# A sixteen-graph network on one core: VectorE centres and scales the normalisations by row blocks, one mask bias tile per graph, and the order of waits

## The chip, the cores and the metric

The kernel runs on one core of one Trainium2 chip. The metric is the device time of one execution in microseconds (us), lower is better. Before the change it is 888.2 us, the median of three runs (886.36 to 890.27).

## The reference

Sixteen graphs of 512 nodes with 64 channels pass four residual layers. `adj` is a dense 512 by 512 matrix per graph, about 6% of it non-zero. Cut to what matters:

```python
def _layernorm(x, axis=-1, eps=1e-05):
    m = jnp.mean(x, axis=axis, keepdims=True)
    v = jnp.var(x, axis=axis, keepdims=True)
    return (x - m) / jnp.sqrt(v + eps)
...
h = jnp.maximum(_layernorm(x, axis=-1), 0.0)
x = x + _L0_gnn_ref(h, adj, ...)   # Chebyshev, 4 orders: three propagations by adj
h = jnp.maximum(_layernorm(x, axis=-1), 0.0)
x = x + _L1_gnn_ref(h, adj, ...)   # encode, two masked attention layers, a 3-layer MLP
h = jnp.maximum(_layernorm(x, axis=-1), 0.0)
x = x + _L2_gnn_ref(h, adj, ...)   # GCN: relu(norm_adj @ h @ kernel)
h = jnp.maximum(_layernorm(x, axis=-1), 0.0)
x = x + _L3_gnn_ref(h, adj)        # adj @ h, then one where it exceeds 0.5, else zero
...
# in an attention layer:
att = softmax(scores * mask - NEG * (1.0 - mask), axis=2)
```

So each graph has four normalisations, each over 64 channels of 512 rows, each followed by a maximum with zero.

## The kernel before

Rows of a graph lie in four blocks of 128 on the 128 partitions (RB = 4). A tile `[P, RB, C]` is 128 partitions by 256 numbers: a row has 64 channels in each of the four blocks.

**Order of the work.** Each engine runs steps in an order written out by hand in the table `ORDER`, one list per engine. An entry `norm_gcn-2` is the step norm_gcn of the graph that entered two rounds ago. A round works on three graphs: the youngest (0) is in the Chebyshev layer, the next (1) in the two attention layers, the oldest (2) in the last attention's end, the MLP, the GCN and the last layer. There are 18 rounds, 14 of them with three graphs. The change leaves three of these lists as they are and takes one entry out of GpSimd's (called POOL in the rows).

The part of VectorE's list (DVE in the rows) that matters, in a round: stats_cheb-0, invert.2-2, norm_cheb-0, split_at0-0 to split_at3-0, attend.2-2, mask0.1-1, mask1.1-1, cheb_ht-0, mask2.1-1, ..., attend.1-1, norm_gcn-2, cheb_fold2-0, gcn_fold-2, stats_last-2, mask0.2-1, cheb_fold1-0, stats_enc-0, norm_last-2, mask1.2-1, norm_enc-0, mask2.2-1, enc_ht-0, mask3.2-1, last_fold-2.

GpSimd's list: norm_cheb-0, add_cheb_bias-0, split_qk.1-1, mask_bias.1-1, inverse_roots-0, cheb_u3-0, norm_gcn-2, mask_bias.2-1, split_qk.2-1, cheb_f0-0, norm_last-2, norm_enc-0, add_mlp_bias-0.

**A normalisation.** VectorE makes mean and variance (`norm_stats`, L685 to L691). GpSimd raises variance plus eps to the power -0.5 (L414, `rstd`), then subtracts the mean from all rows at once (L417, `centred`, 128x256). VectorE then takes the maximum with zero and multiplies by `rstd` in one operation over the 256 numbers of a partition (L698; for the GCN L831, with `rstd` times `dinv` of L828). For the two layers of the young graph (tiles `_pre`) the result is copied once more (L706), so that one transpose on TensorE (L908) puts it on both halves of the partitions. For the two layers of the old graph (tiles `_post`) it is split into a high part in fp32r and a low remainder (`split_u`, L726 and L728), which TensorE multiplies by the adjacency (`propagate`, L936).

**The mask.** `mask_rows` multiplies a block of scores in PSUM by the adjacency (L795), then adds the bias tile `gate` and takes the row maximum in one operation that writes SBUF (L803). `gate` is 0 where there is an edge of weight one and -NEG where there is none: GpSimd makes it from the adjacency (L480, 128x2048), once for each of the two attention layers, though it is the same for both.

**GpSimd's other operations** near them: L428 adds a bias to x (`x_b`), L486 makes the low parts of queries and keys (`q_lo`, `k_lo`), L438 to L448 make roots of the row sums, L454 to L462 the first operand of the propagation, L469 to L474 the sum `f`, which VectorE's cheb_fold1 (L777) waits for, and L501 adds the MLP's bias.

**Transposed adjacency.** TensorE transposes a block of the adjacency (L899), ScalarE copies it out as the high part (L521), VectorE subtracts for the low part (split_at, L712). The two PSUM banks alternate, so the third block's transpose waits for the first L712, the fourth's for the second.

**Waits.** A step names its waits before the instruction. Of several waits the first in the code is held by the instruction itself; the others go to an instruction ahead of it that does nothing but wait. In the rows of instruction order below, the name that stands last in the brackets is the one that the instruction itself holds.

Of the kernel before, what the change touches and what calls it, by code (L numbers as in the profile page):

```python
# [27 lines left out]
P = 128  # L28
# [30 lines left out]
        norm_cheb-0 add_cheb_bias-0 split_qk.1-1 mask_bias.1-1 inverse_roots-0 cheb_u3-0  # L59
        norm_gcn-2 mask_bias.2-1 split_qk.2-1 cheb_f0-0 norm_last-2 norm_enc-0  # L60
# [36 lines left out]
def graph_layers(nc, x, adj, cheb_w, cheb_b, enc_w, enc_b, att_w, att_b, w1, b1, w2, b2, w3, b3,  # L97
# [11 lines left out]
    with ExitStack() as ctx:  # L109
# [58 lines left out]
        h_nat = {"pre": sb("h_nat_pre", [P, RB, 2, C]), "post": sb("h_nat_post", [P, RB, C])}  # L168
# [33 lines left out]
        u2 = sb("u2", [P, RB, C])  # L202
# [50 lines left out]

        var_ready = {t: sem(f"var_ready_{t}") for t in ("pre", "post")}
        h_ready = {t: sem(f"h_ready_{t}") for t in ("pre", "post")}
# [11 lines left out]
        u2_done = sem("u2_done")  # L267
# [3 lines left out]
        dve_post = Chain(sem("dve_post"), 2 * 5 + 3 + 2)  # L271
# [7 lines left out]
        rstd_done = {t: sem(f"rstd_done_{t}") for t in ("pre", "post")}  # L279
# [118 lines left out]
        def _(pool):  # L398
# [51 lines left out]
            def cheb_u3(g):  # L450

                pool.wait_ge(h_ready["pre"], 2 * g.n + 1)
                pool.wait_ge(dinv_done, g.n + 1)
                pool_pre.add(gp.tensor_tensor(u3[:], h_nat["pre"][:, :, 0, :],  # L454
                                              over_blocks(dinv[g.slot][:, 0:RB]), ALU.mult))
                if follows(g):

                    pool.wait_ge(y_ready["pre"], 3 * g.n)
                pool.wait_ge(pool_pre.sem, pool_pre.so_far())
# [6 lines left out]
            def cheb_f0(g):  # L466
# [4 lines left out]
                pool_pre.add(gp.tensor_tensor(c_diff[:], c_diff[:], over_blocks(d_root[:]), ALU.mult))  # L471
                pool.wait_ge(cheb_taken, 3 * g.n + 3)
                pool.wait_ge(pool_pre.sem, pool_pre.so_far())
# [19 lines left out]
            def add_mlp_bias(g):  # L493
# [4 lines left out]
                if g.n >= SLOTS:  # L498
# [6 lines left out]
                    "norm_cheb": scale_norm("pre", 0), "add_cheb_bias": add_cheb_bias,  # L505
                "inverse_roots": inverse_roots, "cheb_u3": cheb_u3, "cheb_f0": cheb_f0, "norm_enc": scale_norm("pre", 1),
                "add_mlp_bias": add_mlp_bias,
                **layer(0, split_qk=queries_keys, mask_bias=mask_bias),
                **layer(1, split_qk=queries_keys),
                **layer(1, mask_bias=mask_bias),  # L510
                "norm_gcn": scale_norm("post", 0), "norm_last": scale_norm("post", 1),
# [3 lines left out]
        def _(act):  # L515
# [66 lines left out]
            def exponent(i):  # L582
                def f(g, a):

                    if i == 0 and follows(g, a):

                        act.wait_ge(inv_done, 2 * g.n + a)
                    act.wait_ge(biased, 8 * g.n + 4 * a + i + 1)
# [46 lines left out]
        def _(dve):  # L635
# [58 lines left out]
            def norm_apply(t, chain, g, k):  # L694

                dve.wait_ge(rstd_done[t], 4 * g.n + 2 * k + 2)
                to = h_nat[t][:, :, 0, :] if t == "pre" else h_nat[t][:]
                one = ve.scalar_tensor_tensor(to, centred[t][:], 0.0, over_blocks(rstd[t][:]),  # L698
                                              ALU.max, ALU.mult)
                if t == "post":  # L700
                    one.then_inc(h_ready[t], 1)
                    return

                chain.add(one)
                dve.wait_ge(chain.sem, chain.so_far())
                ve.tensor_copy(h_nat[t][:, :, 1, :], to).then_inc(h_ready[t], 1)  # L706
# [28 lines left out]
            def cheb_norm(g):  # L735
                if follows(g):

                    dve.wait_ge(ht_ready, 2 * g.n)
                norm_apply("pre", dve_pre, g, 0)
# [45 lines left out]
            def enc_norm(g):  # L785
                norm_apply("pre", dve_pre, g, 1)
# [4 lines left out]
            def mask_rows(g, a, i):  # L791
# [5 lines left out]
                if i == 0:  # L797
                    dve.wait_ge(gate_done, 2 * g.n + a + 1)
# [3 lines left out]
                dve.wait_ge(masked, 8 * g.n + n + 1)  # L802
# [22 lines left out]
            def gcn_norm(g):  # L825

                dve.wait_ge(rstd_done["post"], 4 * g.n + 2)
# [3 lines left out]
                ve.scalar_tensor_tensor(u2[:], centred["post"][:], 0.0, over_blocks(rstd_d[:]),  # L831
                                        ALU.max, ALU.mult).then_inc(u2_done, 1)
                dve.wait_ge(u2_done, g.n + 1)
                split_u("post", dve_post, u2)
# [13 lines left out]
            def last_norm(g):  # L848
                norm_apply("post", dve_post, g, 1)
                dve.wait_ge(h_ready["post"], g.n + 1)  # L850
# [295 lines left out]
```

## Time and profile before

| | |
|---|---|
| median of three runs | 888.2 us |
| lowest, highest | 886.36, 890.27 us |
| the profiled execution | 887.0 us |
| its span, first to last instruction | 885.2 us |
| mean granted TensorE clock | 0.976 of full speed |
| TensorE busy | 768.6 us (87%) |
| VectorE busy | 576.3 us (65%) |
| ScalarE busy | 445.8 us (50%) |
| GpSimd busy | 388.1 us (44%) |

PE is TensorE, DVE is VectorE, ACT is ScalarE, POOL is GpSimd. The profile is of one execution of 887.0 us; outside its span lie 1.8 us. In the steady part a round takes 50.1 us, and all rounds look alike, so one is read below, the one from about 449.6 to 499.7 us.

### The profile page before, as it was taken

To read this page: it belongs to the slowest core of one execution; us is meant where nothing else is said; L and a number is where in the kernel's file an instruction comes from. 1 tells how busy PE (TensorE), PEld (TensorE's weight loads), DVE (VectorE), ACT (ScalarE), POOL (GpSimd) and SP (SyncE) were. 2 spreads that over 40 slices of the span, in tenths; PEclk is the share of its full clock that TensorE was granted. 3 is DMA by queue.
4 is the path that set the end of the run, shared out by engine and by line. 5 is a ranking of instruction groups with operands and counts; after the bars stand their busy time and mean duration, and the time that the engine had idled before them with its cause. 6 is when DMAs were issued, how large, how long until landed. Compare 5 with 4: busy or idle time off the path is not lost.

```text
span 885.2 us, 11494 instructions
## 1 busy us (share of the span) xinstructions
PE 768.6 (87%) x3776; PEld 541.5 (61%) x3808; DVE 576.3 (65%) x1631; ACT 445.8 (50%) x929; POOL 388.1 (44%) x491
## 2 busy tenths in 40 slices
PE   2658799999989899999989999998989999998774
PEld 2435566666766666666766666675766666675543
DVE  3266668577677767677677767667676767765432
ACT  2035645637364654737464553736464563735330
POOL 3134534555353535555353435546263445543301
PEclk9969999999999999999999999999999999999996
DMA  6100100102010100201010100102010010000000
GB/s 168 39 1 0 54 1 5 56 1 59 1 60 1 57 4 0 60 1 60 1 61 1 30 31 0 60 1 61 1 60 0 14 47 1 7 1 7 1 7 6
DMA packets 29276, 22.77 MB, mean 26 GB/s; under 512 B 19488, under 2 KB 21024, under 8 KB 29216
## 3 DMA queue, kind: packets, MB, share of 16 engines
q1 hardware_dynamic: 29216, 22.03, 8.3%
q8 instruction: 31, 0.51, 0.2%
q14 instruction: 29, 0.24, 0.1%
HBM read 19.93 MB, written 2.10 MB: 25 GB/s over the span
## 4 chain that ended last, share of the span: by engine, by line
PE 38%; DVE 22%; POOL 18%; issue 17%; ACT 4%; POOLq 0%; DVEq 0%
PE turn_ps L1056 7%; PE pre_ps L936 5%; PE post_ps L936 4%; POOL rstd_pre L414 4%; DVE u L831 3%; PE turn_ps L1039 3%; POOL rstd_post L414 3%; POOL k_lo L486 2%; DVE h_nat_pre L706 2%; PE pre_ps L899 2%; PE pre_ps L953 2%; POOL centred_pre L417 2%; POOL centred_post L417 2%; DVE score_ps L795 2%; DVE negz L803 2%
## 5 line engine op out<-in xcount | busy, mean ns | idle before, releaser
L589 ACT ACTIVATE negz<-negz,negmax 128x512 f32<-128x512 f32 x128 | 92.3, 721 | 72.0 <-DVE negmax L803 72.0
L414 POOL TENSOR_TENSOR rstd_post<-vareps_post,nhalf 128x4 f32<-128x4 f32 x32 | 32.8, 1026 | 210.1 <-DVE vareps_post L691 210.1
L1056 PE MATMUL turn_ps<-pt,v_n 128*128 128x512 f32 x256 | 115.2, 592 | 0.0
L803 DVE CUSTOM_DVE_ANT_0 negz<-score_ps,gate 128x512 f32<-128x512 f32 x128 | 88.5, 692 | 19.7 <-DVE score_ps L795 6.2
L795 DVE TENSOR_TENSOR score_ps<-score_ps,a_nat 128x512 f32<-128x512 f32 x128 | 89.1, 696 | 17.1 <-PE score_ps L1025 16.1
L936 PE MATMUL pre_ps<-at_hi,u_pair_pre 128*128 128x512 f32 x192 | 87.6, 456 | 7.3 <-DVE u_pair_pre L728 5.2
L414 POOL TENSOR_TENSOR rstd_pre<-vareps_pre,nhalf 128x4 f32<-128x4 f32 x32 | 34.0, 1061 | 131.1 <-DVE vareps_pre L691 131.1
L548 ACT ACTIVATE y_t_pre<-pre_ps 128x512 f32<-128x512 f32 x48 | 28.7, 597 | 123.3 <-PE pre_ps L936 123.3
L596 ACT ACTIVATE pt<-turn_ps 128x512 f32<-128x512 f32 x128 | 74.0, 593 | 15.8 <-PE turn_ps L1039 13.9
L936 PE MATMUL post_ps<-at_hi,u_pair_post 128*128 128x512 f32 x128 | 55.7, 435 | 29.5 <-DVE u_pair_post L728 29.5
L1039 PEld LDWEIGHTS turn_ps<-ident,negz 128*128 128x128 f32 x512 | 61.2, 141 | 32.3 <-issue 16.1
L936 PE MATMUL pre_ps<-at_lo,u_pair_pre 128*128 128x512 f32 x192 | 78.5, 409 | 0.0
L1039 PE MATMUL turn_ps<-ident,negz 128*128 128x128 f32 x512 | 75.7, 275 | 1.8 <-ACT negz L589 1.8
L1056 PEld LDWEIGHTS turn_ps<-pt,v_n 128*128 128x128 f32 x256 | 46.1, 190 | 45.9 <-issue 45.9
L1021 PE MATMUL score_ps<-k_hi,q_hi 128*128 128x512 f32 x128 | 63.1, 493 | 9.5 <-DVE negmax L803 9.5
L486 POOL TENSOR_TENSOR k_lo<-k_t,k_hi 128x512 fp32r<-128x512 f32 x32 | 45.9, 1436 | 55.3 <-ACT k_t L566 55.3
L480 POOL TENSOR_SCALAR gate<-a_nat 128x2048 f32<-128x2048 f32 x32 | 60.9, 1903 | 4.5 <-DVE negmax L803 1.9
L486 POOL TENSOR_TENSOR q_lo<-q_t,q_hi 128x512 fp32r<-128x512 f32 x32 | 43.7, 1366 | 33.4 <-ACT q_t L566 33.4
L899 PE MATMUL pre_ps<-ident,a_nat 128*128 128x128 f32 x256 | 41.2, 290 | 19.6 <-DVE at_lo L712 11.6
L899 PEld LDWEIGHTS pre_ps<-ident,a_nat 128*128 128x128 f32 x256 | 31.5, 148 | 42.0 <-issue 42.0
L814 DVE TENSOR_TENSOR h_t<-turn_ps,inv_row 128x512 f32<-128x512 f32 x32 | 22.1, 692 | 53.0 <-PE turn_ps L1056 53.0
L712 DVE TENSOR_TENSOR at_lo<-pre_ps,at_hi 128x512 fp32r<-128x512 f32 x64 | 42.7, 685 | 21.4 <-ACT at_hi L521 21.4
(137 smaller groups left out, 1815.4 us busy)
## 6 DMA issues: line engine op xcount, KB each, us to landing
a_nat<-in_adj SPq DMA_DIRECT2D x16, 1024.0 KB, 5.8
x_in<-in_x SPq DMA_DIRECT2D x16, 128.0 KB, 2.8
out<-x_out SPq DMA_DIRECT2D x16, 128.0 KB, 1.9
cheb_ws<-in_L_gnn_weight SPq DMA_DIRECT2D x2, 64.0 KB, 4.7
att_w<-in_L_gnn_a_wv SPq DMA_DIRECT2D x2, 64.0 KB, 2.4
att_w<-in_L_gnn_a_wk SPq DMA_DIRECT2D x2, 64.0 KB, 2.2
att_w<-in_L_gnn_a_wq SPq DMA_DIRECT2D x2, 64.0 KB, 2.2
bv_f<-in_L_gnn_a_bv SPq DMA_DIRECT2D x2, 64.0 KB, 2.7
```

Of the source, the lines that this page charges most:

```text
L414: gp.tensor_tensor(rstd[t][:], vareps[t][:], nhalf[:, 0:RB], ALU.pow)\
L480: gp.tensor_scalar(gate[:], a_nat[g.slot][:], -1.0, NEG, ALU.add, ALU.mult)\
L486: gp.tensor_tensor(low[a][:], whole[:], high[a][:].bitcast(F32), ALU.subtract)\
L589: sc.activation(probs[:, i, :], negz[:, i, :], ACT.Exp, bias=negmax[:, i:i + 1], scale=-1.0, accum_out=total[:, i:i + 1]).then_inc(probs_d ...
L596: sc.activation(pt[:, :, i * P:(i + 1) * P], turn_ps[i % 2][:].rearrange("p (j n) -> p j n", n=P), ACT.Copy)\
L795: ve.tensor_tensor(score_ps[i % 2][:], score_ps[i % 2][:], a_nat[s][:, i, :], ALU.mult)\
L803: ve.tensor_tensor_reduce(negz[:, i, :], score_ps[i % 2][:], gate[:, i, :], -1.0, 3.0e38, ALU.add, ALU.min, negmax[:, i:i + 1]).then_inc(b ...
L899: mm = te.transpose(pre_ps[:, j % 2, i * P:(i + 1) * P], a_nat[g.slot][:, i, j * P:(j + 1) * P], ident[:])
L936: mm = te.matmul(bank, u_pair[t][:, j, :, :].rearrange("p a c -> p (a c)"), at[g.slot][:, j, :], start=(j == 0 and at is at_hi), stop=(j = ...
L1021: te.matmul(score_ps[i % 2][:], q_hi[a][:, part], k_hi[a][:], start=True, stop=False)
L1039: mm = te.transpose(turn_ps[i % 2][:, j * P:(j + 1) * P], probs[:, i, j * P:(j + 1) * P], ident[:])
L1056: mm = te.matmul(turn_ps[0][:], v_n[a][:, j * P:(j + 1) * P], pt[:, j, :], start=(j == 0), stop=(j == RB - 1))
```

## The change

- GpSimd's norm steps keep only the power (`root`). VectorE subtracts the mean and multiplies by the scale, in four operations of 128x64, one for each row block, with mean and scale as per-partition scalars (`centre_and_scale`).
- The maximum with zero moves into the operations behind. For the young graph one operation of 512 numbers writes both copies (`norm_pair`). For the old graph the high part is a maximum that writes fp32r, and the low part a maximum and subtraction (`norm_split`). The separate scaling, copy and cast operations go, and so do the tiles `u2` and `h_nat_post`.
- `gate` is made once per graph, not once per layer. The step mask_bias.2-1 goes.
- In eight places the order of waits in the code is changed, and so which of them the instruction itself holds.

```diff
     "gpsimd": """
-        norm_cheb-0 add_cheb_bias-0 split_qk.1-1 mask_bias.1-1 inverse_roots-0 cheb_u3-0
-        norm_gcn-2 mask_bias.2-1 split_qk.2-1 cheb_f0-0 norm_last-2 norm_enc-0
+        norm_cheb-0 add_cheb_bias-0 split_qk.1-1 mask_bias-1 inverse_roots-0 cheb_u3-0
+        norm_gcn-2 split_qk.2-1 cheb_f0-0 norm_last-2 norm_enc-0
         add_mlp_bias-0""".split(),
...
-            def scale_norm(t, k):
+            def root(t, k):
                 def f(g):
                     pool.wait_ge(var_ready[t], 2 * g.n + k + 1)
                     gp.tensor_tensor(rstd[t][:], vareps[t][:], nhalf[:, 0:RB], ALU.pow)\
                         .then_inc(rstd_done[t], 1)
-                    src = {"pre": (x_in[g.slot], x1[g.slot]), "post": (x2, x3)}[t][k]
-                    gp.tensor_tensor(centred[t][:], src[:], meanvar[t][:, :, 0:1].to_broadcast([P, RB, C]),
-                                     ALU.subtract).then_inc(rstd_done[t], 1)
...
-            def mask_bias(g, a):
+            def mask_bias(g):
-                if follows(g, a):
-                    pool.wait_ge(biased, 8 * g.n + 4 * a)
+                if follows(g):
+                    pool.wait_ge(biased, 8 * g.n)
                 gp.tensor_scalar(gate[:], a_nat[g.slot][:], -1.0, NEG, ALU.add, ALU.mult)\
                     .then_inc(gate_done, 1)
...
+            def centre_and_scale(t, chain, src, scale):
+                for i in range(RB):
+                    last_one = ve.tensor_scalar(centred[t][:, i, :], src[:, i, :],
+                                                meanvar[t][:, i, 0:1], scale[:, i:i + 1],
+                                                ALU.subtract, ALU.mult)
+                chain.add(last_one)
                 dve.wait_ge(chain.sem, chain.so_far())
-                ve.tensor_copy(h_nat[t][:, :, 1, :], to).then_inc(h_ready[t], 1)
+            def norm_pair(g, k, src):
+                dve.wait_ge(rstd_done["pre"], 2 * g.n + k + 1)
+                centre_and_scale("pre", dve_pre, src, rstd["pre"])
+                if k == 0 and follows(g):
+                    dve.wait_ge(ht_ready, 2 * g.n)
+                both = centred["pre"][:].unsqueeze(2).to_broadcast([P, RB, 2, C])
+                ve.tensor_scalar(h_nat[:], both, 0.0, None, ALU.max).then_inc(h_ready, 1)
+            def norm_split(chain):
+                chain.add(ve.tensor_scalar(u_pair["post"][:, :, 0, :], centred["post"][:], 0.0, None,
+                                           ALU.max))
+                dve.wait_ge(chain.sem, chain.so_far())
+                ve.scalar_tensor_tensor(u_pair["post"][:, :, 1, :], centred["post"][:], 0.0,
+                                        u_pair["post"][:, :, 0, :].bitcast(F32),
+                                        ALU.max, ALU.subtract).then_inc(u_split["post"], 1)
...
                 ve.tensor_tensor(score_ps[i % 2][:], score_ps[i % 2][:], a_nat[s][:, i, :], ALU.mult)\
                     .then_inc(masked, 1)
-                if i == 0:
-                    dve.wait_ge(gate_done, 2 * g.n + a + 1)
+                dve.wait_ge(masked, 8 * g.n + n + 1)
+                if n == 0:
+                    dve.wait_ge(gate_done, g.n + 1)
                 if follows(g, a):
                     dve.wait_ge(pt_ready, 8 * g.n + n - 3)
-                dve.wait_ge(masked, 8 * g.n + n + 1)
...
             def attend(g, a):
                 to = h3_t if a else h2_t[g.slot]
+                dve.wait_ge(pv_ready, 2 * g.n + a + 1)
                 dve.wait_ge(inv_copied, 2 * g.n + a + 1)
-                dve.wait_ge(pv_ready, 2 * g.n + a + 1)
```

Waits are swapped in the same way in cheb_u3 and cheb_f0 on GpSimd, in exponent on ScalarE, and in cheb_weights and attend on TensorE.

**GpSimd, from the old graph's GCN normalisation to the key's low part of the second attention layer.** Before:

```order
L414 TENSOR_TENSOR rstd_post<-vareps_post,nhalf 128x4 [waits var_ready_post]
L417 TENSOR_TENSOR centred_post<-x,meanvar_post 128x256
L480 TENSOR_SCALAR gate<-a_nat 128x2048 [waits biased]
L486 TENSOR_TENSOR q_lo<-q_t,q_hi 128x512 [waits qkv_done]
L486 TENSOR_TENSOR k_lo<-k_t,k_hi 128x512 [waits qkv_done]
L469 TENSOR_TENSOR c_diff<-c 128x256 [waits c_ready]
```

and with the change:

```order
L412 TENSOR_TENSOR rstd_post<-vareps_post,nhalf 128x4 [waits var_ready_post]
L481 TENSOR_TENSOR q_lo<-q_t,q_hi 128x512 [waits qkv_done]
L481 TENSOR_TENSOR k_lo<-k_t,k_hi 128x512 [waits qkv_done]
L464 TENSOR_TENSOR c_diff<-c 128x256 [waits c_ready]
L466 TENSOR_TENSOR c_diff<-c_diff,d_root 128x256 [waits pool_pre]
```

The centring and the second bias tile are gone between the power and the query's low part.

**VectorE, from the young graph's first normalisation to the first mask of the first attention layer.** Before:

```order
L691 TENSOR_SCALAR vareps_pre<-meanvar_pre 128x4 [waits dve_pre]
L808 RECIPROCAL inv_total<-total 128x4 [waits probs_done]
L698 SCALAR_TENSOR_TENSOR h_nat_pre<-centred_pre,rstd_pre 128x4x64 [waits rstd_done_pre,ht_ready]
L706 COPY h_nat_pre<-h_nat_pre 128x4x64 [waits dve_pre]
L712 TENSOR_TENSOR at_lo<-pre_ps,at_hi 128x512 [waits at_copied] x4
L814 TENSOR_TENSOR h_t<-turn_ps,inv_row 128x512 [waits pv_ready,inv_copied]
L795 TENSOR_TENSOR score_ps<-score_ps,a_nat 128x512 [waits scores_ready]
L803 ISA negz,negmax<-score_ps,gate 128x512 [waits masked,pt_ready,gate_done]
```

and with the change:

```order
L687 TENSOR_SCALAR vareps_pre<-meanvar_pre 128x4 [waits dve_pre]
L815 RECIPROCAL inv_total<-total 128x4 [waits probs_done]
L693 TENSOR_SCALAR centred_pre<-x_in,meanvar_pre,rstd_pre 128x64 [waits rstd_done_pre]
L693 TENSOR_SCALAR centred_pre<-x_in,meanvar_pre,rstd_pre 128x64 x3
L707 TENSOR_SCALAR h_nat<-centred_pre 128x512 [waits ht_ready,dve_pre]
L722 TENSOR_TENSOR at_lo<-pre_ps,at_hi 128x512 [waits at_copied] x4
L821 TENSOR_TENSOR h_t<-turn_ps,inv_row 128x512 [waits inv_copied,pv_ready]
L802 TENSOR_TENSOR score_ps<-score_ps,a_nat 128x512 [waits scores_ready]
L810 ISA negz,negmax<-score_ps,gate 128x512 [waits pt_ready,gate_done,masked]
```

Five operations stand where two stood, with no wait between the first four. The mask's second operation now holds the wait on `masked` itself, and the result of an attention layer holds the wait on `pv_ready`.

## Rows read from the trace of the kernel before

**Rows 1.** The page: busy time, its share of the span, instructions.

```profile
PE 768.6 (87%) x3776; PEld 541.5 (61%) x3808; DVE 576.3 (65%) x1631; ACT 445.8 (50%) x929; POOL 388.1 (44%) x491
```

**Rows 2.** Stretch: length, then busy time (instructions) by engine, clock, DMA.

```profile
450.00:500.00 50.00, 46.42 (x237) 32.99 (x238) 35.61 (x101) 27.62 (x59) 24.13 (x30) 1.00 0.08 27
```

**Rows 3.** Timeline of TensorE, one round: start, length, operation [idle before, releaser].

```profile
452.18 0.50 PE L973 MATMUL pre_ps<-h_t,enc_hi 128*128 128x512 f32 x1 [0.39 <-DVE h_t L720]
...
459.01 1.05 PE L1006 MATMUL qkv_ps<-att_w,h_t 128*128 128x128 f32 x8 [0.85 <-ACT k_t L566]
460.47 1.22 PE L899 MATMUL pre_ps<-ident,a_nat 128*128 128x128 f32 x8 [0.40 <-DVE at_lo L712]
...
467.48 0.50 PE L1021 MATMUL score_ps<-k_hi,q_hi 128*128 128x512 f32 x1 [0.53 <-DVE negmax L803]
...
485.94 0.49 PE L936 MATMUL post_ps<-at_hi,u_pair_post 128*128 128x512 f32 x1 [0.46 <-DVE u_pair_post L728]
...
497.99 0.50 PE L936 MATMUL post_ps<-at_hi,u_pair_post 128*128 128x512 f32 x1 [0.86 <-DVE u_pair_post L728]
```

**Rows 4.** The chain that ended last, in order of time, at two places.

```profile
465.14 0.03 issue
465.19 0.04 issue
465.24 0.69 DVE h_t L814
...
466.57 0.03 issue
466.60 0.05 DVEq L802
466.64 0.08 issue
466.73 0.69 DVE negz L803
...
477.96 0.02 issue
```

**Rows 5.** Timeline of GpSimd in the same round.

```profile
455.88 1.02 POOL L414 TENSOR_TENSOR rstd_pre<-vareps_pre,nhalf 128x4 f32<-128x4 f32 x1 [6.68 <-DVE vareps_pre L691]
456.87 0.62 POOL L417 TENSOR_TENSOR centred_pre<-x_in,meanvar_pre 128x256 f32<-128x256 f32 x1
457.44 0.72 POOL L428 TENSOR_TENSOR x_b<-x_in,cheb_bs 128x256 f32<-128x256 f32 x1
458.12 1.46 POOL L486 TENSOR_TENSOR q_lo<-q_t,q_hi 128x512 fp32r<-128x512 f32 x1
459.54 1.32 POOL L486 TENSOR_TENSOR k_lo<-k_t,k_hi 128x512 fp32r<-128x512 f32 x1
460.94 1.91 POOL L480 TENSOR_SCALAR gate<-a_nat 128x2048 f32<-128x2048 f32 x1
...
482.92 1.90 POOL L480 TENSOR_SCALAR gate<-a_nat 128x2048 f32<-128x2048 f32 x1
```

**Rows 6.** Timeline of VectorE in the same round.

```profile
457.59 0.86 DVE L698 SCALAR_TENSOR_TENSOR h_nat_pre<-centred_pre,rstd_pre 128x256 f32<-128x256 f32 x1 [1.71 <-POOL centred_pre L417]
458.48 1.24 DVE L706 COPY h_nat_pre<-h_nat_pre 128x256 f32<-128x256 f32 x1
...
483.07 2.02 DVE L831 SCALAR_TENSOR_TENSOR u<-centred_post,rstd_d 128x256 f32<-128x256 f32 x1
...
495.60 0.60 DVE L685 BATCH_NORM_STATS2 stats_pre<-x 128x6 f32<-128x64 f32 x4
496.24 0.38 DVE L688 BATCH_NORM_AGGREGATE meanvar_pre<-stats_pre 128x2 f32<-128x6 f32 x4
...
499.31 0.42 DVE L698 SCALAR_TENSOR_TENSOR h_nat_pre<-centred_pre,rstd_pre 128x256 f32<-128x256 f32 x1
499.76 0.29 DVE L706 COPY h_nat_pre<-h_nat_pre 128x256 f32<-128x256 f32 x1
```

More of the change, by code:

```diff
@@ L252, in graph_layers @@
         z_done = sem("z_done")
+        h_ready = sem("h_ready")
         var_ready = {t: sem(f"var_ready_{t}") for t in ("pre", "post")}
-        h_ready = {t: sem(f"h_ready_{t}") for t in ("pre", "post")}
+        rstd_done = {t: sem(f"rstd_done_{t}") for t in ("pre", "post")}
         at_split = sem("at_split")
@@ L270, in graph_layers @@
         dve_pre = Chain(sem("dve_pre"), 2 * 6 + 6)
-        dve_post = Chain(sem("dve_post"), 2 * 5 + 3 + 2)
+        dve_post = Chain(sem("dve_post"), 2 * 7 + 1 + 2)
         gate_done = sem("gate_done")
@@ L278, in graph_layers @@
         qkv_split = sem("qkv_split")
-        rstd_done = {t: sem(f"rstd_done_{t}") for t in ("pre", "post")}
         pool_pre = Chain(sem("pool_pre"), 7 + 4)
@@ L504, in _ @@
             rounds(pool, walk("gpsimd", {
-                    "norm_cheb": scale_norm("pre", 0), "add_cheb_bias": add_cheb_bias,
-                "inverse_roots": inverse_roots, "cheb_u3": cheb_u3, "cheb_f0": cheb_f0, "norm_enc": scale_norm("pre", 1),
+                "norm_cheb": root("pre", 0), "norm_enc": root("pre", 1),
+                "norm_gcn": root("post", 0), "norm_last": root("post", 1),
+                "add_cheb_bias": add_cheb_bias,
+                "inverse_roots": inverse_roots, "cheb_u3": cheb_u3, "cheb_f0": cheb_f0,
                 "add_mlp_bias": add_mlp_bias,
-                **layer(0, split_qk=queries_keys, mask_bias=mask_bias),
+                "mask_bias": mask_bias,
+                **layer(0, split_qk=queries_keys),
                 **layer(1, split_qk=queries_keys),
-                **layer(1, mask_bias=mask_bias),
-                "norm_gcn": scale_norm("post", 0), "norm_last": scale_norm("post", 1),
             }, (pool_pre,)))
@@ L735, in cheb_norm @@
             def cheb_norm(g):
-                if follows(g):
-                    dve.wait_ge(ht_ready, 2 * g.n)
-                norm_apply("pre", dve_pre, g, 0)
+                norm_pair(g, 0, x_in[g.slot])
             def cheb_weights(g):
@@ L785, in enc_norm @@
             def enc_norm(g):
-                norm_apply("pre", dve_pre, g, 1)
+                norm_pair(g, 1, x1[g.slot])
             def mask(i):
@@ L830, in gcn_norm @@
                 dve.wait_ge(dve_post.sem, dve_post.so_far())
[L831 to L834, printed above, removed]
+                centre_and_scale("post", dve_post, x2, rstd_d)
+                norm_split(dve_post)
             def gcn_fold(g):
@@ L848, in last_norm @@
             def last_norm(g):
-                norm_apply("post", dve_post, g, 1)
-                dve.wait_ge(h_ready["post"], g.n + 1)
-                split_u("post", dve_post, h_nat["post"])
+                dve.wait_ge(rstd_done["post"], 2 * g.n + 2)
+                centre_and_scale("post", dve_post, x3, rstd["post"])
+                norm_split(dve_post)
             def last_fold(g):
@@ L904, in turn_h @@
             def turn_h(ready):
-                pe.wait_ge(h_ready["pre"], ready)
+                pe.wait_ge(h_ready, ready)
                 for i in range(RB):
                     mm = te.transpose(pre_ps[:, 0, i * P:(i + 1) * P],
-                                      h_nat["pre"][:, i, :, :].rearrange("p a c -> p (a c)"), ident[:])
+                                      h_nat[:, i, :, :].rearrange("p a c -> p (a c)"), ident[:])
                 mm.then_inc(ht_ready, 1)
```

29 lines of the change are left out of this document (9 added, 20 removed).

## The prediction

> **What bounds the kernel.** I read the page's busy times first: TensorE is busy 87% of the span, VectorE 65%, ScalarE 50%, GpSimd 44% [rows 1]. TensorE is the bound, and the ends of the run hold most of its idle time. In a steady stretch of 50.00 us it is busy 46.42 us at full granted clock [rows 2], so only some 3.5 us of a round can be won by making others faster. The timeline of TensorE shows that they lie in six places [rows 3]: 0.39 us before the encoder (waits for VectorE's h_t), 0.85 before the values (ScalarE's keys), 0.40 before the third transpose of the adjacency (VectorE's at_lo), 0.53 before the third block of scores (VectorE's row maximum), 0.46 before the GCN's propagation and 0.86 before the last layer's (both VectorE's u_pair). Their sum is 3.49. Whatever the change does to GpSimd or VectorE counts only as far as it shortens one of these, or opens a new one. Each engine works its list in order and rounds follow each other without slack elsewhere, so what a place gains or loses counts once per round, about 15 times.
>
> **GpSimd and VectorE disturb each other.** L706 takes 0.29 us at 499.76, where GpSimd does nothing on wide tiles, and 1.24 us at 458.48, where it ends 0.14 us after GpSimd's q_lo; the L698 ahead of it takes 0.86 in place of 0.42 and ends with x_b gone; L831 takes 2.02 us beside the second gate [rows 5, 6]. So a VectorE operation on SBUF tiles stands still until the GpSimd operation that began before it is through. The Trainium skill, "SBUF — State Buffer", section "Who interferes with whom", has this as a lock held for a whole instruction, and counts fp32 tensor_scalar among the operations that need it; the trace agrees for L706's copy (1.24 against 0.29 us), and has no tensor_scalar of this width. It gives a rival below.
>
> **The sum, part by part,** against the profiled execution of 887.0 us (span 885.2 and 1.8 around it), which lies 1.2 under the median of 888.2.
>
> *The GCN's normalisation (old graph).* Before, from the end of the power there pass 0.6 (centring), 0.2 (L828), 2.02 (L831, beside the gate), 0.3 (cast), 0.4 (low part). The centring and the gate go. VectorE gets four 128x64 operations. The trace has none; bounds are the four L688 of six numbers, 0.38 us together, and the four L685, which read 64 numbers one per cycle, 0.60 us [rows 6]. The copy of 256 numbers takes 0.29 where the two-input operation of 256 takes 0.42, 0.13 less, so one-input operations move two numbers per cycle; of the 0.60 that leaves about 0.50, which I take. The maximum in the high part costs what the cast did. The whole is 0.2 + 0.5 + 0.3 + 0.4 = 1.4 us, some 2.1 shorter, against a wait of 0.46: it goes wholly, and VectorE then has 1.6 us in hand. GpSimd next does q_lo, which waits for ScalarE at 485.9 in any case, so nothing is late in its place. 15 x 0.46 = 6.9 us.
>
> *The mask's waits.* Between L795 and the L803 behind it lie 0.03 + 0.05 + 0.08 us with the wait as an instruction of its own (DVEq L802); where an instruction holds its late wait itself, the hop is 0.02 to 0.03 [rows 4]. So each of the eight masks of a graph gets 0.13 us shorter. L814 starts 0.03 + 0.04 + 0.03 after TensorE and gets 0.05 shorter. The wait of 0.53 us has one L814 and one mask in its path: 0.18 x 16 = 2.9 us. The swapped waits of ScalarE, TensorE and GpSimd stand where a wait is early or the step has cover, except that of f on GpSimd (under 0.1 us, beside a mask that ends at the same moment): nothing.
>
> *The young graph's first normalisation.* Before, L706 ends at 459.72, and the first at_lo follows. After, the power ends at 456.90, GpSimd begins x_b at once, and VectorE's four operations wait for it until 457.5. If all four then run in 0.5 us, q_lo follows, 1.3 us, and the pair of maxima (0.43: 0.29 and another 256 numbers at two per cycle; between 0.29 and the 0.69 of a 512-wide operation at one) waits for it and ends at 459.4: 0.3 us earlier than before. Of the wait of 0.40 there goes 0.3: 15 x 0.3 = 4.5 us. Its least value in this case is nothing.
>
> *The last layer's and the encoder's normalisations.* Before, L698 with cast and low part takes 1.2 us, now 0.5 + 0.3 + 0.4 and hops = 1.3: 0.1 more, with the wait of 0.86 behind it. The centring that it no longer needs was done at 496.1, before VectorE arrived, and gave nothing. For the encoder 0.42 + 0.29 become 0.5 + 0.43, 0.2 more, with two masks (0.13 less each) between here and the 0.39 wait. Net 0.1 us per round lost, 1.5 us; the bounds of both prices make it 0 to 0.5 per round, 0 to 7.5 us.
>
> *The second gate.* 1.90 us of GpSimd time goes [rows 5]; GpSimd was idle around it. Beyond L831 it is worth nothing. The first attention layer's gate waits for the same mask as before.
>
> *Start and end,* where nothing covers the chain: two centrings in the last round (0.6 each, less 0.1), and 0.2 to 0.4 in the first graph's two normalisations: 1.6 us.
>
> Sum: 887.0 - 6.9 - 2.9 - 4.5 + 1.5 - 1.6 = 872.6; with the 1.2 to the median 873.8, so **874 us**. Many small operations where one stood also bear a fixed cost each: the Trainium skill, "VectorE: DVE Perf Modes", section "The TRN2 errata — SBUF-src ops pay a fixed extra latency per instruction", advises tiles of 512 and more and gives 58 cycles and one per two elements for such a copy. By it four operations would be an estimated 0.38 us, and the sum about 3 us lower; no row here shows the operation.
>
> **Rivals.**
>
> *1. The four operations and GpSimd's take turns.* The place is the young graph's first normalisation, where GpSimd has x_b, q_lo, k_lo and gate in a row with gaps under 0.1 us [rows 5]. Nothing makes the four operations one: between two lie some 0.06 us in which VectorE asks for nothing. If GpSimd's waiting operation then gets in, one passes before q_lo, one before k_lo, the rest before or behind gate, and the pair of maxima in any case behind gate. Counted from 457.6: 1.35 + 1.3 + 1.95 = 462.2, the maxima end at 462.5, and at_lo starts 2.85 us later than at 459.65. TensorE waits at the third transpose for it. 15 x 2.85 = 43 us lost, and the 4.5 not gained: 872.6 + 4.5 + 43 = 920, on the median's scale 921. It decides if more than 0.5 us of GpSimd's work gets between. For it: GpSimd got in as soon as VectorE paused between L698 and L706 (0.03 us), q_lo running from then on; and q_lo's 1.46 against the 1.3 of k_lo shows that it stood ready. The skill's rule above, one instruction per lock, says the same. Against it: at the change from x_b to q_lo VectorE was let in ahead of an engine that worked without a break; and here no semaphore stands between the four, which are in VectorE's queue together. No row shows two such operations back to back beside GpSimd.
>
> *2. Half of it.* Two operations pass at each gap: two before q_lo, two before k_lo, the maxima before gate, ending at 460.6. at_lo starts 0.9 us late: 872.6 + 4.5 + 13.5 + 1.2 = 892. No change that a measurement can tell.
>
> *3. VectorE becomes the late one.* The four operations cost the 0.60 of L685 and the maxima 0.69, and the first normalisation ends no earlier than before. Then 0.4 per round more are lost at the encoder, 6 us, and up to 4.5 are not gained: about 880 with half of the latter. The long cycle from the keys through f, x1, the last normalisation and the encoder to the values already has three of the six waits in it.
>
> *4. The four do not touch GpSimd at all,* since they run one number per cycle from one input. Then the wait of 0.40 goes wholly: 872.
>
> **How the numbers follow.** A difference of 0.5% (4.4 us) is about what a measurement of this kernel can tell. The forecast and rival 4 get 0.42, rival 3 0.12: faster 0.54. Rival 2: 0.10 for no change. Rival 1: 0.36 for slower. The forecast's own range is 867 to 880; since rival 1 holds more than a fifth, the range must reach it: 867 to 922.
>
> **What would show it.** In the profile after: the four operations of centring together near 0.5 us at all four sites, and not 4 to 5 us at the first of them; L831's successors without 2 us; the gap in front of the mask's second operation at 0.03; TensorE's waits before the GCN's propagation gone and before the third scores at 0.35; a round of 49.2 us in place of 50.1. A round near 52.5 us, with TensorE waiting 3 us at the third transpose, shows rival 1. The prediction is wrong in its mechanism if the first normalisation's operations stretch over q_lo, k_lo and gate.

## The result

The changed kernel takes **951.7 us** (median of 4 runs, 950.3 to 953.3) against 888.4 us before on the same chip: a ratio of 1.071, 95% interval 1.068 to 1.074. It is slower by 63 us, far outside the range of 867 to 922.

Below are the first lines of the page of the changed kernel.

```profile
span 950.3 us, 11638 instructions
...
PE 792.8 (83%) x3808; PEld 555.9 (59%) x3808; DVE 640.9 (67%) x1823; ACT 445.5 (47%) x929; POOL 316.0 (33%) x411
...
PEclk9959999999999999999999989999999999999996
```

Against [rows 1], GpSimd lost 72 us of work and VectorE gained 65, for 192 more instructions. TensorE is 24 us *busier* for about the same work: its matmuls ran slower, so the clock is part of the story. The waits of TensorE over the whole run (line, what it waited for, sum in us, times, longest) show the rest:

```profile
PE pre_ps L904 <- DVE at_lo L722: 48.6, 16, 5.4
PE post_ps L941 <- DVE u_pair_post L714: 35.6, 17, 5.1
```

Before, the first of these (there L899) was 11.6 us and the second (there L936) 29.5. The third transpose of the adjacency costs 37 us more.

A steady round, as in [rows 3, 5, 6], lasts 54.6 us where it lasted 50.1. GpSimd's timeline at the young graph's first normalisation (start, length, operation [idle before, releaser]):

```profile
432.87 1.02 POOL L412 TENSOR_TENSOR rstd_pre<-vareps_pre,nhalf 128x4 f32<-128x4 f32 x1 [8.81 <-DVE vareps_pre L687]
433.86 0.73 POOL L423 TENSOR_TENSOR x_b<-x_in,cheb_bs 128x256 f32<-128x256 f32 x1
434.55 1.26 POOL L481 TENSOR_TENSOR q_lo<-q_t,q_hi 128x512 fp32r<-128x512 f32 x1
435.80 1.27 POOL L481 TENSOR_TENSOR k_lo<-k_t,k_hi 128x512 fp32r<-128x512 f32 x1
437.16 1.95 POOL L475 TENSOR_SCALAR gate<-a_nat 128x2048 f32<-128x2048 f32 x1
```

VectorE's timeline beside it, and then at the GCN's and the last layer's normalisations:

```profile
433.92 3.43 DVE L693 TENSOR_SCALAR centred_pre<-x_in,meanvar_pre,rstd_pre 128x64 f32<-128x64 f32 x4 [1.05 <-POOL rstd_pre L412]
437.38 2.00 DVE L707 TENSOR_SCALAR h_nat<-centred_pre 128x512 f32<-128x512 f32 x1
439.31 1.27 DVE L722 TENSOR_TENSOR at_lo<-pre_ps,at_hi 128x512 fp32r<-128x512 f32 x2
...
463.45 0.98 DVE L693 TENSOR_SCALAR centred_post<-x,meanvar_post,rstd_d 128x64 f32<-128x64 f32 x4
464.47 0.29 DVE L711 TENSOR_SCALAR u_pair_post<-centred_post 128x256 fp32r<-128x256 f32 x1
464.80 0.42 DVE L714 SCALAR_TENSOR_TENSOR u_pair_post<-centred_post,u_pair_post 128x256 fp32r<-128x256 f32 x1
...
476.79 0.98 DVE L693 TENSOR_SCALAR centred_post<-x,meanvar_post,rstd_post 128x64 f32<-128x64 f32 x4
477.80 0.31 DVE L711 TENSOR_SCALAR u_pair_post<-centred_post 128x256 fp32r<-128x256 f32 x1
478.15 0.82 DVE L714 SCALAR_TENSOR_TENSOR u_pair_post<-centred_post,u_pair_post 128x256 fp32r<-128x256 f32 x1
```

The four operations of L693 take 3.43 us here and 0.98 where GpSimd is quiet. They end at 437.35, after x_b, q_lo and k_lo have all run; the maxima of L707, 0.43 us alone, last 2.00 and end 0.27 us after the gate. The four one by one (shortest, middle and longest in ns):

```profile
L693 DVE TENSOR_SCALAR centred_pre<-x_in,meanvar_pre,rstd_pre x4: 304/1010/1343, 433.9 to 437.0; 128x64 f32<-128x64 f32 x4
```

The first three end 0.05 us behind x_b, 0.05 behind q_lo and 0.05 behind k_lo; the fourth, 0.30 us, started before the gate did. That is rival 1. TensorE, in the same stretch:

```profile
440.13 1.94 PE L904 MATMUL pre_ps<-ident,a_nat 128*128 128x128 f32 x8 [3.06 <-DVE at_lo L722]
```

The wait of 0.40 us [rows 3] has become 3.06. The same eight transposes also last 1.94 us where they lasted 1.22. The table by stretches says why (length, then busy time by engine; the third number from the end is the granted clock):

```profile
437.00:440.00 3.00, 0.06 (x1) 0.00 (x0) 2.96 (x5) 0.92 (x3) 2.02 (x2) 0.94 0.44 169
440.00:441.00 1.00, 0.87 (x4) 0.90 (x5) 0.58 (x1) 0.00 (x0) 0.00 (x0) 0.50 0.00 0
...
442.00:443.00 1.00, 1.00 (x3) 0.48 (x2) 0.60 (x2) 1.00 (x4) 0.00 (x0) 0.50 0.00 0
443.00:444.00 1.00, 1.00 (x3) 0.43 (x3) 0.66 (x1) 1.00 (x3) 0.00 (x0) 0.98 0.00 0
```

After 3 us without a matmul the granted clock is 0.50, the lower of its two levels (1.2 GHz), for three microseconds of work. Before, the stretch stood at 1.00 throughout [rows 2]. The other steady rounds show the same fall behind the same wait. In one of them, behind the wait that ends at 549.88, the low clock lasts over 6 us.

**Accounts of the round.** The wait at the third transpose gives +2.66 us, the lower clock +0.7 on the transposes and +0.55 on the attention's matmuls behind them, the last layer's propagation waits 1.77 us where it waited 0.86 (+0.9), the encoder's transposes wait 0.57 more. The GCN's wait of 0.46 is gone, the masks' wait is 0.39 (−0.14), the keys' wait 0.62 (−0.23), the wait before the encoder 0.29 (−0.10). The sum is +4.45 us, against the 4.5 measured. At the encoder's transposes (L913) TensorE did not wait in the rounds before the change.

Two things in this have no place in rival 1: L693 costs 0.98 us even undisturbed, and L714 at the last layer takes 0.82 us where it takes 0.42 at the GCN. The second has this cause in GpSimd's timeline:

```profile
476.96 1.01 POOL L412 TENSOR_TENSOR rstd_pre<-vareps_pre,nhalf 128x4 f32<-128x4 f32 x1 [1.34 <-DVE vareps_pre L687]
477.94 0.75 POOL L496 TENSOR_TENSOR x1b<-x,b_s 128x256 f32<-128x256 f32 x1
```

Since GpSimd no longer centres, x1b starts at once behind the power, runs until 478.69, and L714 ends after it.

### The profile page after: what moved, and what is told of

The parts are those of the page before. It is cut to its first block, busy times and chain, and to the rows that moved or that the text cites. A ratio compares the mean times of both kernels' runs of the same rounds, so it can differ in the third digit from the quotient of the medians.

```text
span 950.3 us, 11638 instructions
## 1 busy us (share of the span) xinstructions
PE 792.8 (83%) x3808; PEld 555.9 (59%) x3808; DVE 640.9 (67%) x1823; ACT 445.5 (47%) x929; POOL 316.0 (33%) x411
## 4 chain that ended last, share of the span: by engine, by line
PE 48%; issue 20%; DVE 16%; POOL 11%; ACT 4%; POOLq 0%; DVEq 0%
PE turn_ps L1061 13%; PE pre_ps L941 7%; DVE centred_pre L693 5%; PE post_ps L941 4%; PE pre_ps L958 3%; POOL rstd_pre L412 3%; DVE h_nat L707 3%; PE pre_ps L904 3%; PE turn_ps L1044 3%; POOL k_lo L481 2%; DVE score_ps L802 2%; PE qkv_ps L995 2%; PE qkv_ps L1000 2%; PE post_ps L1076 2%; PE post_ps L1070 1%
## 5 line engine op out<-in xcount | busy, mean ns | idle before, releaser
L1061 PE MATMUL turn_ps<-pt,v_n 128*128 128x512 f32 x256 | 127.8, 646 | 0.0
L904 PE MATMUL pre_ps<-ident,a_nat 128*128 128x128 f32 x256 | 49.9, 344 | 56.5 <-DVE at_lo L722 48.6
L904 PEld LDWEIGHTS pre_ps<-ident,a_nat 128*128 128x128 f32 x256 | 39.9, 178 | 76.9 <-issue 76.9
L1061 PEld LDWEIGHTS turn_ps<-pt,v_n 128*128 128x128 f32 x256 | 52.5, 217 | 53.5 <-issue 53.5
L481 POOL TENSOR_TENSOR q_lo<-q_t,q_hi 128x512 fp32r<-128x512 f32 x32 | 40.7, 1273 | 78.0 <-ACT q_t L562 78.0
L517 ACT ACTIVATE at_hi<-pre_ps 128x512 fp32r<-128x512 f32 x64 | 39.1, 611 | 57.5 <-PE pre_ps L904 57.5
L693 DVE TENSOR_SCALAR centred_pre<-x_in,meanvar_pre,rstd_pre 128x64 f32<-128x64 f32 x64 | 51.7, 867 | 16.8 <-POOL rstd_pre L412 16.8
```

What stands on the lines that cost most here:

```text
L481: gp.tensor_tensor(low[a][:], whole[:], high[a][:].bitcast(F32), ALU.subtract)\
L693: last_one = ve.tensor_scalar(centred[t][:, i, :], src[:, i, :], meanvar[t][:, i, 0:1], scale[:, i:i + 1], ALU.subtract, ALU.mult)
L904: mm = te.transpose(pre_ps[:, j % 2, i * P:(i + 1) * P], a_nat[g.slot][:, i, j * P:(j + 1) * P], ident[:])
L1061: mm = te.matmul(turn_ps[0][:], v_n[a][:, j * P:(j + 1) * P], pt[:, j, :], start=(j == 0), stop=(j == RB - 1))
```

## The experiments

Theory T: a wide operation on SBUF of either engine runs only when the other's is through, and the waiting engine gets in after each single operation, whatever stands in the other's queue. So the number of operations in which VectorE does the work, and what GpSimd has queued at that moment, would set the loss. Rival theories: the operations are slow in themselves (R1), or the gate and the order of the waits cost something (R2).

### The two other parts of the change alone

To the kernel before, one gate for a graph (e1), the change's order of waits (e2), or both (e3). The diff shows the gate and the mask's waits; the other swaps are those of the change:

```diff
-        norm_gcn-2 mask_bias.2-1 split_qk.2-1 cheb_f0-0 ...
+        norm_gcn-2 split_qk.2-1 cheb_f0-0 ...
...
+                dve.wait_ge(masked, 8 * g.n + n + 1)
-                if i == 0:
-                    dve.wait_ge(gate_done, 2 * g.n + a + 1)
+                if n == 0:
+                    dve.wait_ge(gate_done, g.n + 1)
...
-                dve.wait_ge(masked, 8 * g.n + n + 1)
```

> The kernel before with only the single bias tile per graph. Both theories (turn-taking with GpSimd at the young graph's first normalisation; the four narrow operations cost VectorE too much everywhere) expect the same here: L831 falls from 2.02 to about 0.42 us, TensorE's wait of 0.46 us before the GCN's propagation goes, 15 x 0.46 = 7 us, about 881 us. If the single tile were itself a cause of the loss, the time would be above 888.

> The kernel before with only the order of waits changed. Expected: the gap in front of the mask's second operation falls from 0.16 to 0.03 us, TensorE's wait before the third block of scores from 0.53 to about 0.37; 16 x 0.16 = 2.6 us, about 885.5 us. A swap that puts a late wait on its own instruction somewhere would show as a time at or above 888.

> The single bias tile and the order of waits together, the normalisations as before: the change without its first part. If the parts add, 888.4 - 7 - 2.6 = 879 us, and the first part alone costs 951.7 - 879 = 73 us. If the normalisations only lose together with the other two parts, this kernel is no faster than before.

Measured: e1 879.1 us (ratio 0.991, 0.989 to 0.993), e2 879.7 us (0.992, 0.990 to 0.994), e3 **871.9 us** (0.983, 0.980 to 0.985). R2 falls: both parts are gains, and they add (7.8 and 7.2 against 15.0). The waits gave more than the 2.6 us expected, and so e3 is 7 us below its 879. In e1's round nothing is gone but the GCN's wait of 0.46. In e2 several waits of the round shrink, since the masks stand in more than one path: in e3's round, TensorE's

```profile
444.40 0.50 PE L973 MATMUL pre_ps<-h_t,enc_hi 128*128 128x512 f32 x1 [0.28 <-DVE h_t L720]
...
452.68 1.22 PE L899 MATMUL pre_ps<-ident,a_nat 128*128 128x128 f32 x8 [0.40 <-DVE at_lo L712]
...
459.56 0.50 PE L1021 MATMUL score_ps<-k_hi,q_hi 128*128 128x512 f32 x1 [0.39 <-DVE negmax L803]
```

where 0.39, 0.40 and 0.53 stood [rows 3]. So what the normalisations cost is 951.7 against 871.9: some 79 us by the ratios.

### GpSimd held back during the first normalisation (e4)

The changed kernel, with one wait more ahead of x_b on GpSimd:

```diff
                 if follows(g):
                     pool.wait_ge(x1_done, g.n)
+                pool.wait_ge(h_ready, 2 * g.n + 1)
                 gp.tensor_tensor(x_b[:], ...
```

> The changed kernel, but GpSimd waits with x_b (and so with q_lo, k_lo and gate behind it) until VectorE has finished the young graph's first normalisation. Theory of turn-taking: the first normalisation takes 0.98 + 0.43 us in place of 3.43 + 2.00, the wait of 3.06 us at the third transpose goes, and with it the stretch of granted clock 0.5 behind it (0.7 + 0.55 us): 4.3 us of a round of 54.6, 15 x 4.3 = 64 us, about 887 us. Theory of narrow operations: they stay, and the time stays above 930 us.

Measured: 896.0 us (1.009, 1.007 to 1.012). The groups of L693 in the changed kernel and of the same line, there L694, with GpSimd held (busy us, mean ns of one | idle before):

```profile
L693 DVE TENSOR_SCALAR centred_pre<-x_in,meanvar_pre,rstd_pre 128x64 f32<-128x64 f32 x64 | 51.7, 867 | 16.8 <-POOL rstd_pre L412 16.8
...
L693 DVE TENSOR_SCALAR centred_post<-x,meanvar_post,rstd_d 128x64 f32<-128x64 f32 x64 | 15.7, 310 | 0.6
```

```profile
L694 DVE TENSOR_SCALAR centred_pre<-x_in,meanvar_pre,rstd_pre 128x64 f32<-128x64 f32 x64 | 15.7, 309 | 16.8 <-POOL rstd_pre L412 16.8
...
L708 DVE TENSOR_SCALAR h_nat<-centred_pre 128x512 f32<-128x512 f32 x32 | 13.7, 427 | 1.1
```

867 ns becomes 309, the value of the places without contact, and 56 us are gone at one added wait. R1 falls as the main cause. The expectation was 9 us too low: the last layer's contact with x1b stayed, and in 11 of 14 rounds the clock fell to 0.50 at the matmuls behind the wait of 1.77 to 1.79 us there (below).

### Fewer, wider operations, GpSimd not held (g1, g2)

The line now works on four row blocks at once (g1), or on two (g2). The mean and scale of the first block in each operation are used for all its blocks, so the normalisation is left out in part.

```diff
-                for i in range(RB):
-                    last_one = ve.tensor_scalar(centred[t][:, i, :], src[:, i, :],
+                for i in range(0, RB, 4):
+                    last_one = ve.tensor_scalar(centred[t][:, i:i + 4, :], src[:, i:i + 4, :],
```

> The changed kernel with one operation of 128x256 in place of the four (all row blocks get the first block's mean and scale; the other three blocks' are left out). GpSimd is not held. Turn-taking: one operation passes behind x_b, the maxima behind q_lo, so they end near 0.3 us behind q_lo, 3.3 us earlier than now; TensorE's wait at the third transpose falls from 3.06 to under 0.3 us, the slow stretch behind it goes, and the operation itself costs 0.4 in place of 0.98: about 873 us. If VectorE were simply held until GpSimd's row of operations is through, however many it has, the wait stays near 3 us and the time above 925.

> The same with two operations of 128x128 (each with the scalars of its first block, the others' left out). Turn-taking: one behind x_b, one behind q_lo, the maxima behind k_lo and ahead of gate: 2 us earlier than with four, TensorE's wait near 1 us, about 885 us, between one and four. If the number of operations does not matter: as g1_one_wide.

Measured: g1 **865.1 us** (0.975, 0.972 to 0.977), g2 883.7 us (0.996, 0.994 to 0.997). VectorE's timelines, g1 first:

```profile
446.25 0.81 DVE L693 TENSOR_SCALAR centred_pre<-x_in,meanvar_pre,rstd_pre 128x256 f32<-128x256 f32 x1 [1.05 <-POOL rstd_pre L412]
447.10 1.37 DVE L707 TENSOR_SCALAR h_nat<-centred_pre 128x512 f32<-128x512 f32 x1
```

```profile
455.81 1.97 DVE L693 TENSOR_SCALAR centred_pre<-x_in,meanvar_pre,rstd_pre 128x128 f32<-128x128 f32 x2 [1.05 <-POOL rstd_pre L412]
457.81 1.43 DVE L707 TENSOR_SCALAR h_nat<-centred_pre 128x512 f32<-128x512 f32 x1
```

With one, two and four operations, the maxima end behind q_lo, behind k_lo and behind the gate; TensorE's wait at the third transpose is 0.18, 1.04 and 3.06 us; the time 865, 884 and 952. More operations let more of GpSimd's in ahead. R1 can't make this series of waits: at the places without contact the one operation takes 0.41 us and the two 0.60 together, so the second has 0.19 us of its own and delays the maxima's end by a whole k_lo. The time holds more than this place: of the 19 us between g1 and g2, the wait at the third transpose has 15 × 0.86 = 13, and the waits at the last layer (1.00 for 0.80) and the encoder's transposes (0.19, none in g1) the other 6; of the 68 from g2 to the changed kernel it has 15 × 2.02 = 30, and the rest is the lower clock behind it and the longer waits at the last layer (1.77 for 1.00) and the encoder's transposes (0.57 for 0.19). In g1 and g2 the clock stays at 1.00 at the transposes. g1 is 8 us faster than the 873 expected, g2 1 us faster than its 885.

### Immediates in place of the per-partition scalars (f1)

The kernel with GpSimd held, with 0.0 and 1.0 for mean and scale in L694, so the centring and scaling are left out:

```diff
-                                                meanvar[t][:, i, 0:1], scale[:, i:i + 1],
+                                                0.0, 1.0,
```

> e4_hold with the numbers 0 and 1 in place of the two per-partition scalars (mean and scale are left out of all four normalisations). If it is the reading of per-partition scalars from SBUF that makes four 128x64 operations take 0.98 us, they fall to about 0.50 (a start every 0.10 us), some 1.2 us per round are saved at the last layer's and the encoder's normalisation: 896 - 18 = 878 us. If it is the fixed cost of a short operation, they stay at 0.98 and the time at 896.

Measured: 868.4 us (0.978, 0.975 to 0.981).

```profile
L694 DVE TENSOR_SCALAR centred_pre<-x_in 128x64 f32<-128x64 f32 x64 | 8.0, 191 | 16.2 <-POOL rstd_pre L412 16.2
```

191 ns in place of 309, and four in a row 0.50 us in place of 0.98. The prediction's other estimate for the four, 0.38 us, is below both. The prediction's 0.50 us is what this operation costs *with immediates* (numbers in the instruction itself); with the two scalars read from SBUF for each partition it costs 0.12 us more, four times per normalisation. The gain over the kernel with GpSimd held, 27.5 us where 18 were expected, is more than 0.48 us at the last layer and the encoder in each round would give (some 14): VectorE now also reaches the last layer's low part ahead of x1b (0.43 us there, not 0.82), and the clock no longer falls behind the wait there.

### x1b held until the last layer's low part is done (f3)

The kernel with GpSimd held, and x1b later:

```diff
+                if g.n >= 2:
+                    pool.wait_ge(u_split["post"], 2 * (g.n - 1))
                 gp.tensor_tensor(x1b[g.slot][:], ...
```

> e4_hold with GpSimd's x1b held back until VectorE has the last layer's low part (L714, 0.82 us beside x1b, 0.43 alone). If this collision, which came with GpSimd's missing centring, costs what the row shows: 15 x 0.4 = 6 us, about 890 us. If the wait is covered: 896.

Measured: 883.3 us (0.994, 0.993 to 0.996), 12.7 us less than with GpSimd held alone, of which the shorter wait is 15 × 0.39 = 6, as expected; the rest, which the expectation had not, is clock. The wait before the last layer's propagation is 1.39 us, and in all 14 rounds the matmuls behind it start 0.23 us apart:

```profile
444.48 0.51 PE L944 MATMUL post_ps<-at_hi,u_pair_post 128*128 128x512 f32 x1 [1.39 <-DVE u_pair_post L717]
444.82 0.40 PE L944 MATMUL post_ps<-at_lo,u_pair_post 128*128 128x512 f32 x1
445.05 0.40 PE L944 MATMUL post_ps<-at_hi,u_pair_post 128*128 128x512 f32 x1
```

### The first normalisation alone as before (i1)

The changed kernel, with GpSimd centring and VectorE's single operation and copy at that one place:

```diff
+                    if (t, k) == ("pre", 0):
+                        gp.tensor_tensor(centred[t][:], x_in[g.slot][:], ...
...
-                norm_pair(g, 0, x_in[g.slot])
+                dve_pre.add(ve.scalar_tensor_tensor(to, centred["pre"][:], 0.0,
+                                                    over_blocks(rstd["pre"][:]), ALU.max, ALU.mult))
```

> The changed kernel with the young graph's first normalisation alone as before (GpSimd centres, VectorE has one operation of maximum and scale and the copy); the other three normalisations as in the change. Theory: nearly all of the loss is at that place. What is left over the 871.9 us of the kernel with gate and waits alone is the x1b contact at the last layer and the four operations at 0.98 in place of 0.50 us: 872 + 15 x (0.9 or less) = 880 to 886 us, and no stretch of a round at half the granted clock. Rival (the three other places bear a good part of the loss, by what they push GpSimd to do): over 900 us.

Measured: 900.3 us (1.014, 1.012 to 1.015). The expectation missed by 14 us or more; its rival, over 900, is met. From it to the changed kernel are 51 us, the first normalisation's; from e3 to it are 28, so the three others do bear a good part. Its timeline at the last layer's propagation shows what the expectation had left out:

```profile
451.08 0.49 PE L954 MATMUL post_ps<-at_hi,u_pair_post 128*128 128x512 f32 x1 [1.78 <-DVE u_pair_post L719]
451.42 0.57 PE L954 MATMUL post_ps<-at_lo,u_pair_post 128*128 128x512 f32 x1
451.78 0.63 PE L954 MATMUL post_ps<-at_hi,u_pair_post 128*128 128x512 f32 x1
452.21 0.63 PE L954 MATMUL post_ps<-at_lo,u_pair_post 128*128 128x512 f32 x1
```

```profile
450.00:451.00 1.00, 0.00 (x0) 0.00 (x0) 0.97 (x3) 0.00 (x0) 0.75 (x2) 1.00 0.00 0
...
452.00:453.00 1.00, 1.00 (x3) 0.79 (x3) 1.00 (x6) 0.59 (x1) 0.00 (x0) 0.50 0.00 0
```

The wait is 0.96 us longer than e3's 0.82 in every round. In this round a granted clock of 0.50 follows it, and the matmuls start 0.43 us apart instead of 0.23. This happens in 7 of 14 rounds, in the others the eight run at 0.23; a round with the fall lasts 51.48 us, one without 50.72, where e3 has 49.04. So the lower clock costs 0.76 us in such a round, some 5 us of the run. The rest is the longer wait, and one of 0.57 us before the encoder's transposes, which e3 doesn't have, in the rounds in which the clock holds. In the changed kernel the same wait of 1.77 or 1.78 us stands before the same matmuls, and there the clock fell in one round of 14 (at 535 us, from the seventh of the eight matmuls on). With GpSimd held it fell in 11 of 14, and with x1b held, behind the wait of 1.39, in none. What selects, these runs don't settle.

### Could the order of GpSimd's list do better?

To e3, x_b before the centring, where GpSimd is idle (h1), and besides q_lo held until the normalisation is done (h2):

```diff
-        norm_cheb-0 add_cheb_bias-0 split_qk.1-1
+        add_cheb_bias-0 norm_cheb-0 split_qk.1-1
...
+                    if (t, k) == ("pre", 0):
+                        pool.wait_ge(h_ready["pre"], 2 * g.n + 1)
```

> The kernel before with one gate and the wait order of the change (871.9 us measured), and x_b put ahead of the young graph's first centring in GpSimd's list, where GpSimd is idle. Theory (the lock is held for a whole operation, and whoever waits gets it next): x_b no longer stands in the way of L698, but q_lo now begins in its place as soon as the centring is through, so L698 waits 1.3 us for it and the copy L706 1.3 us for k_lo; VectorE's first at_lo starts 0.5 to 0.8 us later than now, the wait at the third transpose grows from 0.40 to about 1.0, and the time is 872 + 15 x 0.6 = 881 us. Rival (contact costs what overlaps in bytes, not in turns): one wide GpSimd operation less beside L698 is 0.4 us less in each round, 866.

> As the run before (x_b ahead of the centring), and GpSimd's q_lo waits until VectorE has the normalisation and its copy done. Theory: L698 takes 0.42 and L706 0.29 us there instead of 0.86 and 1.24, the first at_lo starts 1.4 us earlier than now, q_lo 0.3 us later. The wait of 0.40 at the third transpose goes whole: 872 - 15 x 0.40 = 866 us. Rival: q_lo, k_lo and the gate, 0.3 us later, are what the scores wait for, and the gain is given back: 872.

Measured: h1 882.9 us (0.995, 0.993 to 0.996), h2 869.3 us (0.979, 0.977 to 0.980). h1 is *slower* than e3, though GpSimd has one wide operation less beside the normalisation. VectorE and then GpSimd:

```profile
455.35 1.40 DVE L698 SCALAR_TENSOR_TENSOR h_nat_pre<-centred_pre,rstd_pre 128x256 f32<-128x256 f32 x1 [1.71 <-POOL centred_pre L417]
456.78 1.25 DVE L706 COPY h_nat_pre<-h_nat_pre 128x256 f32<-128x256 f32 x1
```

```profile
455.21 1.26 POOL L486 TENSOR_TENSOR q_lo<-q_t,q_hi 128x512 fp32r<-128x512 f32 x1
456.58 1.30 POOL L486 TENSOR_TENSOR k_lo<-k_t,k_hi 128x512 fp32r<-128x512 f32 x1
```

L698 ends behind q_lo and L706 behind k_lo, one each, and the wait at the third transpose is 0.94 us (expected: 1.0). The short x_b had been a shield: what matters is the length of the operation that one stands behind. The rival to T, bytes rather than turns, gave 866 and falls. That the time met the expected 881 within 2 us is in part luck: besides the 0.54 us at the third transpose, h1 has a wait of 0.29 us before the encoder's transposes that e3 hasn't and that the expectation had not seen. It comes, as in h2 below, from x_b's new place behind x1b.

h2 gains 0.4% over e3 by the ratios, about 3.5 us where 6 were expected. The wait at the third transpose is 0.19 us, but x_b now runs early, behind x1b, beside the encoder's copy, which takes 0.71 in place of 0.29 and makes the encoder's transposes wait 0.29:

```profile
442.08 0.71 DVE L708 COPY h_nat_pre<-h_nat_pre 128x256 f32<-128x256 f32 x1
...
442.85 0.66 PE L910 MATMUL pre_ps<-ident,h_nat_pre 128*128 128x128 f32 x4 [0.29 <-DVE h_nat_pre L708]
```

Of the versions that leave nothing out of the computation it is the fastest.

## Why the prediction was wrong

**What bounds the kernel: right in the main.** TensorE's waits decide, and most of the loss stands at two of the six places that were named. The third place, the encoder's transposes (0.57 us), was not among them.

**The step that failed** is the one on the young graph's first normalisation: "If all four then run in 0.5 us, q_lo follows". It took the four operations, which have no semaphore between them, for one. They are four, and GpSimd gets in between the first and second and between the second and third: 3.43 us in place of the 0.5 behind x_b, with the maxima behind the gate. The wrong evidence was given weight: that no semaphore stands between them did not keep GpSimd out, and the row that did speak (q_lo in at the pause of 0.03 us between L698 and L706) was in hand. Rival 1's mechanism was right: it had the first at_lo 2.85 us later than before, and from the end of the power to it the trace has 5.42 us (439.31 less 433.89) against 2.75, which is 2.67 more. The Trainium skill, "SBUF — State Buffer", section "Who interferes with whom", has a lock for a whole instruction, and h1's 1.40 and 1.25 us agree with it; the reading of it as the rival, which had a chance of 0.36 against the forecast's 0.42, was the right one.

**Rival 1's price was too low**, 921 for 952, since three terms were missing or mis-sized:
- *The clock.* Nothing in the prediction had a price for what a wait does to the matmuls behind it. Shown: 1.25 us in the round above behind the third transpose's wait (0.7 + 0.55), 2.7 in the round with the long low stretch, and 20 us in the 13 rounds between 160 and 830 us. TensorE's busy time, 24 us more for about the same work, fits that.
- *The four operations at 0.50 us.* They take 0.98. The price came from operations without per-partition scalars; f1 has 0.50 with immediates and so shows where the other half comes from. The upper bound of 0.60 was too low as well. It costs at the last layer's and the encoder's normalisations, about 0.5 us each; at the encoder it makes the new wait of 0.57 us.
- *x1b.* The prediction said that GpSimd's centring there "was done at 496.1, before VectorE arrived, and gave nothing". As a step it gave nothing, but it kept x1b 0.6 us later. Its removal puts x1b on L714: 0.4 us per round, 6 us. These two make up the step of the wait there from 0.86 to 1.77 us: 0.5 + 0.4. For both normalisations and their contacts the sum had 1.5 us; the runs have 28 for the three other normalisations together (i1 less e3).

**The gate: right** (6.9 us predicted, 7.8 measured). **The mask's waits: mis-sized**, 2.9 predicted and 7.2 measured; the wait of 0.53 was priced, while the same masks lie ahead of L973 and of the last layer's propagation too. Those three waits are 0.31 us shorter in e2, its round 0.43; no run parts the eight swaps. **One operation for the maxima: right**, 0.43 us. **The GCN's normalisation: right in its effect.** The four take 0.98 us in place of 0.5, but had 1.6 us in hand there, and the wait is gone all the same.

By the measured parts: 888.4 − 15.0 (gate and waits) + 28 (three normalisations, the clock in it) + 51 (the first one, the clock in it) = 952.4. The parts are differences between the runs, so they must close; what they show is how the loss divides.

## What to carry to other kernels

Splitting one VectorE operation into several is not neutral while GpSimd has work queued: count the gaps, let up to one of GpSimd's operations into each, and price the sum by the *length* of those operations. When work is taken from an engine, ask what it will do earlier in its place, and on which operations of its neighbour that falls. And price a new wait of TensorE of some microseconds by the matmuls behind it as well, at the lower clock.

## What was not expected of the hardware

- A tensor_scalar of 128x64 takes 0.19 us with immediates (f1) and 0.31 with two scalars per partition from SBUF; of 128x256 it takes 0.41 with them (g1). Four of 64 cost 0.98 us together, one of 256 0.41.
- Behind TensorE's wait of 1.39 us the clock stayed at 1.00 in every round; behind 1.78 us it fell to 0.50 in 1 of 14 rounds of the changed kernel, in 7 of i1 and in 11 of e4; behind 3.06 us it fell each time, mostly for some three microseconds of work and once for over six. What selects at the middle length stays open.
- A wait that is an instruction of its own in front of the mask's second operation cost about 0.13 us (VectorE idle for 0.16 to 0.17 us there before, 0.03 in e3). The eight swaps, by which the operation itself holds the late wait and which change no operation, were together worth 0.8% of the time (e2).
